# Attention heads on one Trainium2 core: the first maxima product of each pair of steps is issued directly behind its scores, ahead of the value products

## The reference, cut to what matters

```python
scores = jnp.einsum('bhqd,bhkd->bhqk', q, k) * scale        # 4 batches x 16 heads, 1024 x 1024
scores = jnp.where(causal[None, None], scores, -jnp.inf)
att = jax.nn.softmax(scores, axis=-1)
y = jnp.einsum('bhqk,bhkd->bhqd', att, v)
```

## Time and profile before

| | |
|---|---|
| median of 3 runs | 1196.34 us (1195.28 to 1199.88) |
| profiled execution | 1202.0 us, span of the trace 1200.3 us |
| mean granted TensorE clock | 0.897 of full speed |
| busy over the span: PE, weight loads, DVE, ACT, POOL | 83%, 60%, 64%, 56%, 42% |
| exponentials of the scores (line 1814) | 576, 601 ns each |
| reductions of maxima (line 1842) | 384 in two groups, 1015 and 821 ns each |

### The profile page before, as it was taken

How to read it: one execution, slowest core, us unless ns; L and a number is a source line. 1 busy time by engine, 2 the same in 40 slices (tenths; PEclk the granted TensorE clock), 3 DMA queues, 4 the chain that set the end, 5 groups by cost and what they waited for, 6 DMA issues and landing times. The chain is left out here.

```text
span 1200.3 us, 25180 instructions
## 1 busy us (share of the span) xinstructions
PE 993.4 (83%) x9046; PEld 722.6 (60%) x9046; DVE 767.0 (64%) x1557; ACT 675.0 (56%) x1595; POOL 508.3 (42%) x692
## 2 busy tenths in 40 slices
PE   5226999999789967999999999999887299999930
PEld 1125788787778854555555555555546178888830
DVE  3995444444377637888888888888617844444437
ACT  2733445444357522777787877878737545555410
POOL 1535667675455540222232323323210067777720
PEclk9757999999579985999999999999969689999975
DMA  8723555553447554345464553544219423333349
GB/s 305 229 97 98 191 196 202 198 182 136 154 135 249 178 157 90 73 106 123 98 148 104 113 119 95 122 103 102 57 45 344 162 84 105 103 102 106 98 140 315
DMA packets 100582, 172.94 MB, mean 144 GB/s; under 512 B 16240, under 2 KB 64368, under 8 KB 100464
## 3 DMA queue, kind: packets, MB, share of 16 engines
q1 hardware_dynamic: 86640, 133.57, 38.9%
q0 software_dynamic: 13824, 37.77, 9.2%
HBM read 101.55 MB, written 69.47 MB: 142 GB/s over the span
## 5 line engine op out<-in xcount | busy, mean ns | idle before, releaser
L1814 ACT ACTIVATE spare<-h_psS 128x512 f32<-128x512 f32 x576 | 306.6, 601 | 92.8 <-PE h_psS L1724 90.5
L1842 DVE TENSOR_REDUCE h_part<-h_psM 128x2 f32<-128x1024 f32 (+3 forms) x256 | 249.1, 1015 | 11.5 <-PE h_psM L1703 10.9
L1877 POOL TENSOR_SCALAR_AFFINE_SELECT spare<-spare 128x256 f32<-128x256 f32 x256 | 99.5, 407 | 303.7 <-ACT spare L1814 303.7
L886 PE MATMUL m_psG<-wgu,m_x_hi 128*128 x576 | 195.0, 420 | 1.2 <-DVE m_x_lo L960 1.2
L864 POOL DMA_INDIRECT ys<-m_y,m_slot_u x144 | 142.3, 988 | 78.4 <-ACT m_y L951 53.5
L1751 PE MATMUL h_psO<-spare,a_VP 128*17 128x256 f32 (+3 forms) x3072 | 167.0, 337 | 8.9 <-ACT spare L1805 8.7
L1703 PE MATMUL h_psM<-h_KT,h_QT 48*128 48x512 f32 (+3 forms) x768 | 146.2, 423 | 22.5 <-DMA h_QT<-a_QD 14.8
L1724 PE MATMUL h_psS<-h_QT,h_KT 49*128 49x512 f32 (+3 forms) x768 | 159.2, 407 | 3.0 <-ACT spare L1814 2.3
L858 POOL DMA_INDIRECT m_xg<-xn,m_slot_u x140 | 135.7, 969 | 47.8 <-issue 22.3
L970 DVE TENSOR_TENSOR m_h<-m_act_g,m_psG 128x256 f32<-128x256 f32 x144 | 60.6, 421 | 136.1 <-ACT m_act_g L944 136.1
L886 PE MATMUL m_psY<-wdn,m_h_hi 128*128 x576 | 128.5, 304 | 10.8 <-issue 6.5
(11 more groups left out here) (230 smaller groups left out, 1570.4 us busy)
## 6 DMA issues: line engine op xcount, KB each, us to landing
xn<-spare SPq DMA_DIRECT2D x16, 512.0 KB, 5.8
wg_d<-wgu SPq DMA_DIRECT2D x16, 512.0 KB
p_yg<-ys SPq DMA_DIRECT2D x16, 512.0 KB, 5.5
a_KD<-spare SPq DMA_DIRECT2D x32, 256.0 KB, 3.0
h_KT<-a_KD SPq DMA_DIRECT2D x64, 128.0 KB
h_QT<-a_QD SPq DMA_DIRECT2D x64, 128.0 KB
a_OD<-spare SPq DMA_DIRECT2D x128, 64.0 KB, 2.5
wgu<-wg_d SPq DMA_DIRECT2D x16, 512.0 KB, 10.5
```

What stands on the lines that cost most here:

```text
L886: m = pe.matmul(out, s[:, c, :], ww[:, bass.ds(at + c * width, width)], start=(n == 0), stop=(n == 3 * CC - 1))
L1814: act.activation(prob[k % NP][:, h, :], psS[x % NS][:, :], ACT.Exp).then_inc(s_read, 1)
L1842: m = dve.tensor_reduce(out, psM[k % NM][:, :, at:at + n], AX.X, ALU.max, negate=True)
L1877: m = pool.affine_select(block, block, [[0, 2], [1, P]], ALU.is_ge, 0.0, 0, -1)
```

## The change

Each group's first new step now has its M directly behind its S, ahead of the group's V; the second new step's M stays behind its S. So the V of the group lie between the two M, where both M stood behind them. No instruction is added or taken away, and the other engines' orders are the same.

```diff
                         for k in new[0:1]:
                             scores(k)
+                            ahead(k)
                         for k in ks:
                             values(k)
                         for k in new[1:]:
                             scores(k)
-                        for k in new:
                             ahead(k)
```

## The result

| | before | changed |
|---|---|---|
| median, range | 1198.11 us (4 runs, 1195.28 to 1205.3) | 1224.78 us (4 runs, 1221.07 to 1226.8) |
| ratio, 95% interval | | 1.0197 (1.0165 to 1.0228) |
| profiled execution, its span | 1202.0, 1200.3 | 1221.07, 1219.3 |
| a pair of heads, typical | 12.50, every fourth 13.28 | 13.54, all |
| pair 30, without M | 12.30 | 12.30 |

The ratio on 1198.11 is +23.6 us (19.8 to 27.3); forecast were +23.7, and 1220 in the range 1206 to 1237. Both medians together give +26.7.

What follows compares the result with a forecast made beforehand. Bound: the loop of S, ACT's exponential and the freed tile, with M free only inside 1.18 us behind an S. 29 pairs x 1.01 = 29.3 us, less 5.6 for reciprocals, gives +23.7: 1220 us, range 1206 to 1237.

Steps and rivals of the forecast that it cites:

- S6 to V4: M4 between the late S7 and V4 costs a full M: 0.33 us more a pair.
- S8 to V6: M6 in front of V6 costs a full M: 0.33 us more a pair.
- S4 to S6: M0 leaves the S4 to S5 gap, M2 comes behind the row product before V2: net 0.34 us more a pair.
- S1 to V8: M6 leaves the gap, M8 comes before V8: V8 at 2.00 us behind S1 instead of 1.62, 0.38 more.
- V8 to V0: M8 leaves this stretch and M0 fills the wait before V0: 1.37 us instead of 1.74, a gain of 0.37.
- M beside the late head: M4 behind the second head's late S7: nothing of it hidden, the full 0.33 us paid before V4.
- the first rival: M slips in beside the late head, half or less of each exposed: +2.5 us at a half, 1199; chance 6%.
- The row product: Between S5 and V2: waits for S4's second exponential, 1.68 us behind S4 instead of 1.75, so 0.07 won.
- The hole in front of V0: PE loses 0.43 us a pair before V0 waiting for ACT's output copy; M0 fills it.
- The reciprocals: DVE's reciprocal behind M4's reduction no longer delays M7: 0.80 us less in each of seven pairs, -5.6 us.
- No waits of M on DVE: M4 starts some 3 us after M2, whose tile takes 1.7 to fill and reduce: no new PE waits on DVE.
- the third rival: The clock falls from added holes of 0.3 to 0.5 us, four a pair: 80 us on top, 1300; chance 3%.

Runs made afterwards that it cites:

- e5: Kernel before with each exponential over 384 of 512 columns: a pair 12.17 us, total 1190.7 us (kernel before beside it 1207.6).
- e6: Changed kernel with each exponential over 384 of 512 columns: a pair 13.05 us, total 1207.3 us (kernel before beside it 1207.6).
- e8: Changed kernel with the row product behind M2 instead of ahead of it: a pair 13.16 us, total 1213.8 us (kernel before beside it 1207.6).
- e12: Changed kernel with ACT's output copy between the two exponentials of S2: a pair 13.54 us, total 1296.0 us (kernel before beside it 1276.6).
- e9: e1 with each DVE reduction over half its columns: a pair 12.50 to 12.57 us, total 1265.6 us (kernel before beside it 1276.6).
- e1: Kernel before with only M0 moved ahead of its group's V: a pair 13.11 us, total 1218.2 us (kernel before beside it 1195.8).
- e4: Kernel before with only M8 moved ahead of its group's V: a pair 13.1 us, total 1217.3 us (kernel before beside it 1195.8).
- e3: Kernel before with only M4 and M6 moved ahead of their groups' V: a pair 13.61 us, total 1232.4 us (kernel before beside it 1195.8).
- e2: Kernel before with only M2 moved ahead of its group's V: a pair 13.41 us, total 1233.2 us (kernel before beside it 1195.8).

## Why the prediction was right, point by point

- **What bounds the stage.** Right. The floor of 1.18 to 1.19 us stands in the changed kernel at four places, and e5 and e6 move it from ACT's side alone.
- **The sum for a pair.** 1.01 forecast, 1.04 measured, but the terms did not all come out. Misses of 0.07 to 0.10 downward in three of them and of 0.21 and 0.09 upward in the other two nearly cancel, so that the sum is this close is partly luck:

| | before | changed | forecast | measured |
|---|---|---|---|---|
| S6 to V4 | 1.61 | 1.84 | +0.33 | +0.23 |
| S8 to V6 | 1.61 | 1.85 | +0.33 | +0.24 |
| S4 to S6 | 2.94 | 3.49 | +0.34 | +0.55 |
| S1 to V8 | 1.62 | 1.93 | +0.38 | +0.31 |
| V8 to V0 | 1.74 | 1.46 | -0.37 | -0.28 |

- **M beside the late head** was mis-sized: 0.10 of the 0.33 of a lone M is hidden, not half as in the first rival and not nothing as in the forecast. The rule of the Trainium skill on row groups ("TensorE: Matmul & The Clock Gate", section "Packing small matmuls — row/col tiling") points the right way, and the trace has M4 start with the late S7, at 671.15; but the second head's S7 and M4 still come one after the other, 0.33 us each, and V follows at 671.81. At V8 it is more: behind the late S2 the forecast had 0.41 until M8, and it took 0.24 (677.05 is 1.42 behind S1).
- **The row product** was the step that failed. It was priced at its place before, inside V2. M2 now stands between the two and it runs alone: 668.47 - 668.15 = 0.32 us; V2 V3 without it take 1.00 instead of 1.17. That is 0.15, and M2 at 0.50 instead of 0.41 is another 0.09: together the miss of 0.21 in S4 to S6. e8 gives a part of that back.
- **V behind M** costs more than M itself: M2 to V2 is 0.50 and M8 to V8 0.51, where M8 to S3 was 0.41. The same in front of V0 (678.46 to 679.02, 0.56 instead of the 0.47 taken) is why the gain at the turn was 0.28 and not 0.37.
- **The hole in front of V0** is filled, as said; e12 shows that nothing of it is left, e9 that M0 alone fills it free of charge once it does not wait for DVE.
- **The reciprocals** gave back 7 x 0.80 = 5.6 us as forecast.
- **No waits of M on DVE** was right for the whole change, but for a reason that the prediction only touched: that the M alternate everywhere. e1 to e4, where they don't, lost 0.6 to 1.1 us a pair, in e1 all of it to just this, and my expectations for them left it out.
- **The clock** did not fall in the middle: 1.00 with four waits a pair, of up to 0.7 us for a weight load, in which PE itself was idle for about 0.2 us at a time. The holes of 0.3 to 0.5 us that the third rival counted on did not come. What the Trainium skill tells of micro-idles that make the clock oscillate (same page, section "A second HAM failure mode: psum-queue depth-cycling") the changed kernel does not show. e1 shows what it would cost: one idle time of 1.22 us, the clock down to 0.91 and 0.84 in the two stretches that hold it, and two pairs 14.55 and 15.04 us long instead of 13.91 and 12.77. So the rival was a real one, in a kernel with longer waits. What brings it on stays open: an idle time of 0.65 us stands in front of a fall once (e4), and 0.65 in all its other places and 0.77 in the seven pairs with a reciprocal of e5 stand in front of none.

## What to carry to other kernels

When an engine's share is high but taking its work away (here pair 30) leaves the time as it was, look for the loop: producer, consumer, buffer freed, next producer. Its length is a floor; work fits below it for nothing, and work moved out of it to another place on the in-order engine is paid for (here 0.23 of 0.33 us at least, unless it lands in another hole). Price a reordering as a whole: with two buffers, spacing decides, and the parts tried one by one cost three times what they cost together.

## What the runs showed of the hardware that was not expected

- The two heads' products run beside each other and each head keeps its own time: with the second head held back to 671.15, M4's first head started with it, and V came 0.66 later instead of 0.43 + 0.33.
- The last pair has the same products in all 14 profiled executions, one of each kernel. Before, e1 and e3 ran it in 14.4 to 14.5 us at 0.53 of the clock and e2 in 14.07 at 0.58, the other ten at full clock (10.04 to 10.06 us with full exponentials). Kernels without the change are on both sides; those with the whole change (also e6, e8 and e12) were all at full clock, so a part of the change in this is not ruled out. That the same kernel goes both ways was not seen, as each has one profile. What decides it stays open.
- A clock at half speed for 3.4 to 6.8 us came behind PE idle times of 0.65, 0.88 and 1.22 us (e4, e4, e1), and did not come behind 0.65 us in the other pairs with a reciprocal, nor behind 0.77 us in those of e5.
